# Narrow attention steps: the whole query between the second and third score tile, eight value matmuls in a row, and the transposes of the rest behind the projection

## The reference

```python
xn = x * rsqrt(mean(x * x, -1) + eps) * norm_w
q  = (xn @ wq).reshape(B, T, 4, 4, 32)              # 4 groups of 4 heads
k, v = cond @ wk, cond @ wv                          # 4 groups, 77 rows
attn = softmax(einsum('btgrd,bsgd->bgrts', q, k) / sqrt(32))
out  = einsum('bgrts,bsgd->btgrd', attn, v)
x    = x + out.reshape(B, T, 512) @ wo
```

## Time and profile before

| | |
|---|---|
| median of 3 runs | 2021.42 us (2021.1 to 2021.67) |
| profiled execution | 2020.28 us, span 2018.5 us |
| PE busy | 1993.4 us (99%), 11482 matmuls |
| PE weight loads | 1738.1 us (86%) |
| DVE busy | 1434.6 us (71%) |
| ACT busy | 985.6 us (49%) |
| POOL busy | 646.2 us (32%) |
| chain that ended last | PE 50%, issue 31%, POOL 13%, DVE 4% |

### The profile page before, as it was taken

One profiled execution on the slowest core, in us unless ns is written; L12 is line 12 of the kernel. 1 busy time (PEld: TensorE's weight loads), 2 busy tenths in 40 slices (PEclk: granted clock), 3 DMA queues, 4 the chain that ended last, 5 costly groups with the idle time before them and its releaser, 6 DMA issues.

```text
span 2018.5 us, 31330 instructions
## 1 busy us (share of the span) xinstructions
PE 1993.4 (99%) x11482; PEld 1738.1 (86%) x11482; DVE 1434.6 (71%) x2488; ACT 985.6 (49%) x1814; POOL 646.2 (32%) x518
## 2 busy tenths in 40 slices
PE   8999999999999999999999999999999999999998
PEld 8999988888888887888888888888888878888887
DVE  4423367777777767888888677776777677888886
ACT  3222255444544554655555454444455555555553
POOL 0000043222222255554444332222222354443441
PEclk9999999999999999999999999999999999999999
DMA  8789742222222223343333332222222232333332
GB/s 236 150 174 212 188 92 63 78 62 62 67 78 63 65 75 96 103 112 98 89 100 96 82 111 66 62 67 78 62 63 70 79 89 72 100 95 87 86 74 85
DMA packets 262538, 191.02 MB, mean 95 GB/s; under 512 B 197522, under 2 KB 199986, under 8 KB 259826
## 3 DMA queue, kind: packets, MB, share of 16 engines
q1 hardware_dynamic: 262386, 189.03, 36.8%
HBM read 132.66 MB, written 56.26 MB: 94 GB/s over the span
## 4 chain that ended last, share of the span: by engine, by line
PE 50%; issue 31%; POOL 13%; DVE 4%; ACT 1%; SPq 0%; DMA 0%; POOLq 0%; DVEq 0%; ACTq 0%
POOL prob L1405 6%; PE acc_bank L900 6%; PE ctx_bank L270 4%; PE t_bank L878 4%; PE ctx_bank L271 4%; PE ctx_bank L272 4%; POOL x_s L1380 4%; PE q_bank L856 3%; PE q_bank L858 3%; PE q_bank L860 3%; PE acc_bank L270 3%; PE acc_bank L272 3%; PE acc_bank L271 3%; PE s_bank L270 2%; POOL rest L1414 2%
## 5 line engine op out<-in xcount | busy, mean ns | idle before, releaser
L1405 POOL TENSOR_TENSOR prob<-prob,rinv 128x1232 f32<-128x1232 f32 x128 | 288.3, 2252 | 1010.4 <-DVE rinv L1255 1010.4
L856 PE MATMUL q_bank<-x_s,w_s 128*128 128x512 f32 x768 | 315.6, 411 | 0.8 <-POOL w_s L1398 0.8
L860 PE MATMUL q_bank<-x_s,w_s 128*128 128x512 f32 x768 | 307.1, 400 | 0.0
L858 PE MATMUL q_bank<-x_s,w_s 128*128 128x512 f32 x768 | 307.0, 400 | 0.0
L270 PE MATMUL acc_bank<-o_s,w_s 128*128 128x512 f32 x752 | 304.5, 405 | 2.2 <-DVE o_s L1246 2.2
L272 PE MATMUL acc_bank<-o_s,w_s 128*128 128x512 f32 x752 | 294.4, 392 | 0.0
L271 PE MATMUL acc_bank<-o_s,w_s 128*128 128x512 f32 x752 | 293.4, 390 | 0.0
L1069 ACT ACTIVATE s_bank<-bias_s 128x308 f32<-128x308 f32 x256 | 109.9, 430 | 361.2 <-DVE prob L1217 361.2
L1213 DVE TENSOR_REDUCE mx<-s_bank 128x4 f32<-128x308 f32 x512 | 241.6, 472 | 61.5 <-PE s_bank L272 49.3
L900 PE MATMUL acc_bank<-pT_s,vals_s 128*128 128x512 f32 x1024 | 280.4, 393 | 3.5 <-DVE pT_s L1232 3.5
L1084 ACT ACTIVATE prob<-prob,rstd 128x308 f32<-128x308 f32 x256 | 141.3, 553 | 279.9 <-DVE prob L1217 251.1
(11 more groups left out here) (107 smaller groups left out, 4136.4 us busy)
## 6 DMA issues: line engine op xcount, KB each, us to landing
stream<-x_back SPq DMA_DIRECT2D x128, 256.0 KB, 2.7
x_front<-stream SPq DMA_DIRECT2D x96, 256.0 KB, 3.4
x_back<-stream SPq DMA_DIRECT2D x96, 256.0 KB, 3.5
kvw_raw<-kvw SPq DMA_DIRECT2D x17, 1024.0 KB, 8.6
k_scr<-k_out SPq DMA_DIRECT2D x36, 308.0 KB, 9.8
keys_s<-k_scr SPq DMA_DIRECT2D x128, 77.0 KB, 2.4
v_scr<-v_out SPq DMA_DIRECT2D x8, 1024.0 KB
vals_s<-v_scr SPq DMA_DIRECT2D x512, 6.5 KB
```

What stands on the lines that cost most here:

```text
L856: pe.matmul(out, w[0], x_now[0], start=k == 0, stop=False)
L858: pe.matmul(out, w[0], x_now[1], start=False, stop=False)
L860: mm = pe.matmul(out, w[1], x_now[0], start=False, stop=k == XC - 1)
L1405: pool.tensor_tensor(view, view, rinv[:, slot].unsqueeze(2).broadcast_to([P, TILES * GH, CTX]), ALU.mult).then_inc(p_norm, 1)
```

## The change

In narrow steps whose number in the layer is 3 or higher (`unbroken`: steps 35 to 63 and 99 to 127) the order is another. PE issues both halves of the query between score tiles two and three, all eight value matmuls in a row, then sets 0 and 1, the projection, and the rest. VectorE subtracts the rest of unit s-2 at the head of step s instead of at the end of step s-1 (`rest_later`), then the four tiles and the addition, the query, the sums and their inverse, the output, set 0, set 1. ScalarE takes the query between the two pairs of exponentials and the output ahead of set 0, and the rest last, behind the new input and the weights. Wide steps keep their order. The instructions are the same in kind and number.

```diff
--- before.py
+++ after.py
@@ -188,9 +188,13 @@
 
         return u - UNITS * (u // (2 * UNITS)) + 1
 
+    def unbroken(self, s):
+
+        return s < NU and kind(s).name == "B" and s % UNITS > 2
+
     def rest_later(self, u):
 
-        return kind(u).name == "A" and u + 2 < NU and kind(u + 2).name == "A"
+        return self.unbroken(u + 1) or kind(u).name == "A" and u + 2 < NU and kind(u + 2).name == "A"
 
     def biased(self, u, t):
         return TILES * (u - UNITS * (u // (2 * UNITS))) + t + 1
@@ -1016,18 +1020,23 @@
                     run(q, half)
                     if plan.stats_at(s) is not None:
                         stats(plan.stats_at(s))
+                    if plan.unbroken(s):
+                        run(q, half)
                     if plan.behind(s):
                         project(*projections.pop(0))
                     run(scores(s, 2), 1)
                     run(scores(s, 3), 1)
-                    run(v, 3)
+                    run(v, 8 if plan.unbroken(s) else 3)
                     turned(0)
                     run(q, half)
                     run(v, 9)
                     turned(1)
-                    turned(2)
+                    if not plan.unbroken(s):
+                        turned(2)
                     for item in projections:
                         project(*item)
+                    if plan.unbroken(s):
+                        turned(2)
                 elif s == NU:
                     run(v, 9)
                     for item in projections:
@@ -1190,18 +1199,26 @@
                 else:
                     if s < NU:
                         exps(s, 0)
+                        if plan.unbroken(s):
+                            next(q, None)
                         exps(s, 1)
                     bias(s + 1, 0)
                     bias(s + 1, 1)
+                    if plan.unbroken(s):
+                        split_o(s - 2, 0)
                     turned(0)
                     next(q, None)
                     next(q, None)
-                    for m in range(pv):
-                        split_o(s - 2, m)
+                    if not plan.unbroken(s):
+                        for m in range(pv):
+                            split_o(s - 2, m)
                     turned(1)
-                    turned(2)
+                    if not plan.unbroken(s):
+                        turned(2)
                     fresh_x()
                     weights()
+                    if plan.unbroken(s):
+                        turned(2)
 
         @block.vector
         def _(dve):
@@ -1339,6 +1356,8 @@
                     if s >= 1 and not plan.rest_later(s - 1):
                         rest_t(s - 1, TWICE)
                 else:
+                    if s >= 2 and plan.rest_later(s - 2):
+                        rest_t(s - 2, TWICE)
                     if s < NU:
                         for t in range(TILES):
                             tile_scores(s, t)
@@ -1354,16 +1373,23 @@
                         add_result(*projections.pop(0))
                         denominators(s)
                         turned(0)
+                    elif plan.unbroken(s):
+                        next(q, None)
+                        denominators(s)
+                        rest_o(s - 2, 0)
+                        turned(0)
                     else:
                         turned(0)
                         if s < NU:
                             denominators(s)
                     next(q, None)
                     next(q, None)
-                    for m in range(pv):
-                        rest_o(s - 2, m)
+                    if not plan.unbroken(s):
+                        for m in range(pv):
+                            rest_o(s - 2, m)
                     turned(1)
-                    turned(2)
+                    if s >= 1 and not plan.rest_later(s - 1):
+                        turned(2)
                     for item in projections:
                         if item not in plan.late(s):
                             add_result(*item)
```

## The result

The changed kernel took 2035.18 us (median of 4 runs, 2034.16 to 2036.97) against 2021.26 us before (4 runs, 2019.89 to 2021.67): a ratio of 1.0071, 95% interval 1.0055 to 1.0087. It is slower by 14 us, and the forecast was 2037.6. The span of the profiled execution is 2033.2 us for 2018.5.

The account below looks back on a forecast made before the run. PE was taken as bound, within 0.13 us of its 10.35 us plain-step floor. VectorE's late signals add 5.0 (plain), 5.7 (first projections), 4.2 (statistics), 0.3 and 1.0 (last steps): +16.2, giving 2037.6 us; own range 2031 to 2042.

Parts of the forecast that it names:

- named bounds: Limits for two estimated intervals: VectorE's addition to query (0.54 and 0.70 us), PE's transposes behind their weight load (0.03 and 0.11).
- Third tile at T+3.62: On PE, the third score tile starts 3.62 us after T, the step's first score matmul; 1.4 us later than before.
- VectorE's chain of 5.88 to the end of set 0: VectorE's seven intervals from taking up tile three at T+4.24 sum to 5.88 us, ending at T+10.12.
- Plain steps 10.65, first projections 10.84, statistics 11.09: Forecast lengths in us of the narrow steps, 10.48 or 10.46, 10.43 and 10.79 before; +5.0, +5.7 and +4.2 in all.
- First projection late by 0.49: In steps numbered 1, the tenth projection matmul waits for the output of unit s-2, starting at 9.72 instead of 9.23.
- The rest's subtraction at the head costs nothing: At the next step's head, VectorE's second-tile subtraction ends at T+3.50; tile four's load is due at 3.9, 0.4 spare.
- rival (3): ScalarE copies the rest's transposes late, behind input splits and weights; steps lose up to 0.6 us each; 2046; 8%.
- The last narrow step +1.0: Very last narrow step, without query between tiles two and three: the head's subtraction delays it by 0.9; +1.0 us.
- rival (4): Clock falls to its lower level for some new pauses; one step at half clock costs 10 us, two give 2058; 2%.
- The last narrow step before a wide layer +0.3: That step's closing transposes of the rest are the same 0.30 us late; +0.3 us.
- What would show it: Signs: forecast step spacings; PE waits of over 10 us on pT_s, some 7 on o_s, none of scores on prob.
- The gain that was to be had: PE's distance from its floor: 0.13 + 0.08 + 0.11 + 0 = 0.32 us in four steps, under 5 us in all.

Follow-up runs that it names:

- e1: Changed kernel with VectorE's set 0 subtraction put ahead of the output's remainder in the 58 steps; 2033.74 us, ratio 1.0061 to the kernel before.
- e2: Changed kernel with VectorE's output remainder and set 0 both ahead of the sums and their inverse; 2037.31 us, ratio 1.0079 to the kernel before.
- e3: e2 plus GpSimd adding squares ahead of its multiplication in steps numbered 2; 2022.23 us, ratio 1.0007 to the kernel before.
- e7: Kernel before, with seven instead of six query matmuls between tiles two and three, from the fourth step on without statistics; 2017.19 us, ratio 0.9978.
- e6: e3 with new-input loads ahead of weight loads in the DMA queue and the very last narrow step in old order; 2019.17 us, ratio 0.9989.
- e8: Changed kernel, but the very last narrow step keeps its old order; 2034.16 us, ratio 1.0067 to the kernel before.
- e4: Changed kernel with PE's transposes of the rest back ahead of the projection, nothing else; 2227.02 us in one run.

## Why the prediction was right

The time lay 2.4 us under the forecast and inside its own range; the mechanism and its place are those of the working, and the sizes nearly. Part of the closeness is luck: the regular steps cost 3.7 us less than the sum had, and a fall of the clock in the last step, which the sum did not have, gave 1.6 back. The named bounds (0.54 and 0.70, 0.03 and 0.11) would give about 2034 to 2046, not the 2031 to 2042 that was written; the time lies in both.

- *Third tile at T+3.62, VectorE's chain of 5.88 to the end of set 0.* Measured 3.69 from a record that starts early by 0.07, and 960.22 to 966.07, 5.85. The one interval without a row, addition to query, was put at 0.60 and is 0.60 (962.02 to 962.62). e1 and e2 show by intervention that this chain, and nothing in PE's order, sets the step's end.
- *Plain steps 10.65, first projections 10.84, statistics 11.09.* Measured 10.59, 10.78 and 11.05. The transposes start at T+10.21 as forecast, but two errors cancel in that: T is here a record that starts 0.07 early, and from VectorE's taking up tile three to the transposes it is 5.90 (960.22 to 966.12), where the working has 5.88 + 0.09 = 5.97. The chain is 0.03 shorter, and the transposes start with their waiting load instead of 0.04 behind it. The next record follows 0.38 after them, which is 0.45 without the same 0.07, for 0.44. Together the step is 0.06 shorter, in 56 steps 3.4 us, nearly the whole of the difference: the regular steps cost +11.2 us for +14.9.
- *First projection late by 0.49.* The tenth matmul starts 0.52 behind the ninth (975.62, 976.14), 0.29 beyond its slot, and its successor another 0.10 beyond (not shown: 976.47): 0.39 by these starts, 0.42 by the mean length (10.78 less 10.36), so this term was some 0.07 too large.
- *The rest's subtraction at the head costs nothing.* Right: VectorE's fourth-tile signal comes in time in all regular steps but one. In step 42 the copies on ScalarE are late as rival (3) has it, and the step is 10.74; in e2 and e3 the same place costs 1.7 to 2.0 us in steps 38 and 42 (ScalarE's wait for the input ahead of step 42 is 1.49 us in the changed kernel and 2.68 in e3). The working spoke of this subtraction as moved. In VectorE's order it is not: the end of one narrow step and the head of the next are the same place, with nothing between.
- *The last narrow step +1.0.* The order cost 1.2. The half clock of rival (4) did come, once, for some matmuls in this step, at 1.6 us and not 10: I had priced a whole step. All four runs of the changed kernel have a mean granted clock of 0.999 and all four of e1 1.000, so the fall is probably not of the profiled execution alone.
- *The last narrow step before a wide layer +0.3.* It was 0.2: 1116.94 to 1130.28 for 13.13 before.
- *What would show it.* The forecast named the view of PE's waits with over 10 us for the transposes. That view has 2.4 us; the view of the weight loads has 23.2 (3.9 before). For the projection on o_s it named some 7 us, and the weight loads have 10.9 for 3.2. Waits of scores on prob were to be none; the weight loads have 4.7 us for 3.5 before, step 42 and the last step being what is new. The view was wrong there, the waits were not.

The gain that was to be had, at most 0.32 us in four steps, is confirmed by e7, which takes 0.26 of it: 3.6 us in the 56 steps of the trace, 4.2 by the medians.

## What to carry to other kernels

When an engine is within a per cent of its floor, measure the wait before moving work around it: 0.14 us wanted one matmul of 0.23, and six of them pushed the other engine's chain past the next bank's turn. An instruction that is moved later on the bound engine moves everything that the helper engine does behind it; so sum the helper's chain from that point to the next signal that the bound engine needs, and order the helper by who is waited for first (set 0 and output ahead of a 1.5 us reduction whose reader has a step of slack). A position that makes one wait disappear can be paid for by the third engine in line, as GpSimd's squares were in e2.

## What the runs showed of the hardware

The granted clock fell behind short pauses, but not each time. In the changed kernel PE stood still for 1.6 us between 1998.4 and 2000.0 and the clock of 2001.43 to 2005.65 is 0.60, with matmuls of 512 columns 0.43 us apart, that is 1.2 GHz, instead of 0.23 at 2.4 GHz; in e2 the clock behind the same pause is 0.67 (2004.25 to 2008.50); in e1, e3, e6 and e8 the same pause was followed by 1.00. So it fell in two of six profiled executions, and e6 has one more fall at 317.0, behind a pause of 1.27 us. In e4 with its 2.80 us in each step some stretches stay at 1.00 and others fall:

```profile
888.69:915.37 26.68, 21.08 (x114) 17.81 (x113) 17.71 (x32) 14.38 (x27) 11.71 (x9) 1.00 0.33 91
2144.21:2175.33 31.12, 25.52 (x114) 21.03 (x113) 17.71 (x32) 9.71 (x18) 4.50 (x2) 0.84 0.19 46
```

Both hold two steps with the same 114 matmuls and the same waits; the second is 4.4 us longer. The page "TensorE: Matmul & The Clock Gate" of the Trainium skill tells (section "A second HAM failure mode: psum-queue depth-cycling") of a clock that alternates under short pauses between groups of matmuls. By that, e4 with its 2.80 us agrees; the regular steps of the changed kernel, with 0.2 to 0.5 us of pause each, do not (1.00 throughout).
